# A decoder block's attention stage: the context's local sums and their rounded halves at another place in the step, and the integer transposes of the up projection at another place in the queue

## What is computed

```python
x = _layernorm(x + _L0_attn_ref(x, Wqkv, Wout, Wgate, bgate, decay_param))   # causal linear attention
x = _layernorm(x + _L0_xattn_ref(x, ctx_1024, ctx_1024))                     # decayed sum of ctx*ctx over the blocks
x = _layernorm(x + _L0_ffn_ref(x, w_gate, w_up, w_down))                     # quantised gated FFN
# _L0_attn_ref: q, k = elu + 1; running sums with a decay per head; out = q * running_kv / den;
#               g = sigmoid(out @ Wgate.T + b); (g * out + (1 - g) * v) @ Wout.T
# _L0_xattn_ref: r = 0.9 * r + (k * v)[t] along the first axis of (16, 512, 512); out = q * r
```

## Time and profile before

| | us |
|---|---|
| median of 3 runs | 2640.48 |
| lowest, highest | 2638.88, 2640.67 |
| profiled execution | 2641.53 |
| its span, first to last instruction | 2639.8 |
| TensorE busy (matmul) | 2550.7 (97%) |
| VectorE busy | 2020.0 (77%) |
| ScalarE busy | 1356.8 (51%) |
| mean granted TensorE clock | 0.983 of full |

### The profile page before, as it was taken

One profiled execution on the slowest core, in us unless ns is written; L12 is line 12 of the kernel. 1 busy time (PEld: TensorE's weight loads), 2 busy tenths in 40 slices (PEclk: granted clock), 3 DMA queues, 4 the chain that ended last, 5 costly groups with the idle time before them and its releaser, 6 DMA issues.

```text
span 2639.8 us, 32066 instructions
## 1 busy us (share of the span) xinstructions
PE 2550.7 (97%) x11218; PEld 2132.8 (81%) x11218; DVE 2020.0 (77%) x2838; ACT 1356.8 (51%) x1727; POOL 397.1 (15%) x281
## 2 busy tenths in 40 slices
PE   7999999999999997999999999999999699999998
PEld 6888888888888886888888887888888588888887
DVE  7899999999999895555555458987777766666665
ACT  4455555555555555333333358888888522222222
POOL 0000000000000000000000003422222143333332
PEclk9999999999999998999999999999999899999999
DMA  4011222211211224555555559777777635555552
GB/s 175 9 64 72 83 100 91 76 72 72 80 72 68 84 112 153 182 191 191 189 183 185 183 172 314 272 262 256 258 258 260 243 152 213 211 211 211 212 211 115
DMA packets 146714, 429.85 MB, mean 163 GB/s; under 512 B 73184, under 2 KB 81632, under 8 KB 106976
## 3 DMA queue, kind: packets, MB, share of 16 engines
q1 hardware_dynamic: 143920, 412.39, 43.0%
q10 hardware_dynamic: 2736, 16.78, 1.6%
HBM read 235.67 MB, written 177.21 MB: 156 GB/s over the span
## 4 chain that ended last, share of the span: by engine, by line
PE 57%; DVE 2%; DMA 1%; ACT 1%; issue 1%; SPq 0%; POOL 0%; POOLq 0%; ACTq 0%; DVEq 0%
PE pair L1999 12%; PE pair L2001 12%; PE pair L2000 12%; PE pair L2058 6%; PE pair L2059 6%; PE pair L2060 6%; DMA ff_q<-x_ints 0%; PE pair L2009 0%; DVE ff_gs L1722 0%; DMA ff_gs<-gate_ints 0%; DMA up_products<-ff_group 0%; DVE ff_up_max L1745 0%; DVE ff_up_abs L1727 0%; DVE ff_lo L1917 0%; ACT ff_group L1504 0%
## 5 line engine op out<-in xcount | busy, mean ns | idle before, releaser
L1999 PE MATMUL pair<-ff_hi,wide_h 128*128 128x512 f32 x1536 | 599.7, 390 | 3.0 <-ACT ff_group L1504 2.8
L2001 PE MATMUL pair<-ff_hi,wide_l 128*128 128x512 f32 x1536 | 598.3, 390 | 0.0
L2000 PE MATMUL pair<-ff_lo,wide_h 128*128 128x512 f32 x1536 | 598.3, 390 | 0.0
L1504 ACT ACTIVATE ff_group<-pair,ff_scales 128x512 f32<-128x512 f32 x384 | 257.2, 686 | 304.1 <-PE pair L2001 293.0
L1999 PEld LDWEIGHTS pair<-ff_hi,wide_h 128*128 128x128 f32 x1536 | 288.7, 188 | 64.2 <-ACT ff_group L1504 3.2
L2001 PEld LDWEIGHTS pair<-ff_hi,wide_l 128*128 128x128 f32 x1536 | 288.7, 188 | 60.4
L2000 PEld LDWEIGHTS pair<-ff_lo,wide_h 128*128 128x128 f32 x1536 | 288.7, 188 | 59.4
L2058 PE MATMUL pair<-wide_h,ff_hi 128*128 128x512 f32 x768 | 299.7, 390 | 24.4 <-DVE ff_lo L1911 23.5
L935 PE MATMUL pair<-xh,wide_h 128*128 128x512 f32 x768 | 309.2, 403 | 12.3 <-DVE wide_l L543 11.7
L939 PE MATMUL pair<-xh,wide_l 128*128 128x512 f32 x768 | 307.0, 400 | 0.0
L936 PE MATMUL pair<-xl,wide_h 128*128 128x512 f32 x768 | 306.7, 399 | 0.0
(11 more groups left out here) (235 smaller groups left out, 4622.6 us busy)
## 6 DMA issues: line engine op xcount, KB each, us to landing
gate_products<-ff_group SPq DMA_DIRECT2D x48, 1024.0 KB, 4.0
ff_raw<-gate_products SPq DMA_DIRECT2D x48, 1024.0 KB, 5.7
up_products<-ff_group SPq DMA_DIRECT2D x48, 1024.0 KB, 4.4
ff_raw<-up_products SPq DMA_DIRECT2D x48, 1024.0 KB, 9.2
gate_ints<-ff_gs SPq DMA_DIRECT2D x48, 512.0 KB, 2.7
ff_gs<-gate_ints SPq DMA_DIRECT2D x48, 512.0 KB, 9.9
xt_raw<-in_xT SPq DMA_DIRECT2D x64, 256.0 KB, 3.5
csq<-in_ctx_rows SPq DMA_DIRECT2D x16, 1024.0 KB, 7.3
```

What stands on the lines that cost most here:

```text
L1504: act.activation(group[:, g, m * T:(m + 1) * T], out_ps[(GM * g + m) % 6][:], ACT.Copy, scale=s_x).then_inc(evacuated, 1)
L1999: pe.matmul(o, wh[:, m, k], hi[:, par, k], start=(k == 0), stop=False)
L2000: pe.matmul(o, wh[:, m, k], lo[:, par, k], start=False, stop=False)
L2001: mm = pe.matmul(o, wl[:, m, k], hi[:, par, k], start=False, stop=(k == KC - 1))
```

## The change

On ScalarE the copy into `csq_h` goes from the middle of the step to its end, behind `normalise(0, s)`; the copy into `rec_turned` goes ahead of `split_x(s+1, (2, 3))`. On VectorE `local_sums(s+1)` goes from behind `split_x(s+1, (0, 1))` to behind `second_residual`, and `last_sum_low(s+1)` to the very end of the step, behind `scale_difference(s+1, 0)`. On TensorE `turn_reciprocals` goes three matmuls earlier in projection tile 3. On SyncE each up step used to issue the transpose for the next step at its group 0; now it issues the one for the step after next at its group 1, behind the store of the group's products. No arithmetic is added or removed, apart from two unread warm-up matmuls in step 0.

```diff
@@ scalar, step
                     if front:
-                        act.wait_ge(summed, (TT - 1) * (s + 1))
-                        if back:
-                            act.wait_ge(carry_ready, s)
-                        act.activation(csq_h[:], csq[:, 1 - par, TT - 1], ACT.Copy).then_inc(sqh_ready, 1)
+                        act.wait_ge(turned_ready, s + 1)
+                        act.activation(rec_turned[:], turn_bank, ACT.Copy).then_inc(rec_turned_ready, 1)
                     if nxt:
                         split_x(s + 1, (2, 3))
-                    if front:
-                        act.wait_ge(turned_ready, s + 1)
-                        act.activation(rec_turned[:], turn_bank, ACT.Copy).then_inc(rec_turned_ready, 1)
                     if back:
                         squares(0, s, (2, 3))
...
                     if back:
                         normalise(0, s)
+                    if front:
+                        act.wait_ge(summed, (TT - 1) * (s + 1))
+                        if back:
+                            act.wait_ge(carry_ready, s)
+                        act.activation(csq_h[:], csq[:, 1 - par, TT - 1], ACT.Copy).then_inc(sqh_ready, 1)
@@ vector, step
                     if nxt:
                         split_x(s + 1, (0, 1))
-                    if front:
-                        local_sums(s + 1, 1 - par)
...
                     if nxt:
                         split_x(s + 1, (2, 3))
-                    if front:
-                        last_sum_low(s + 1, 1 - par)
...
                     if back:
                         second_residual(s, par)
+                    if front:
+                        local_sums(s + 1, 1 - par)
                     if piece is not None and piece + 1 < NPIECE:
                         piece_scales(piece + 1)
                     if front:
                         scale_difference(s + 1, 0)
+                        last_sum_low(s + 1, 1 - par)
@@ tensor, step
-                        project(s, (3,), lambda k: turn_reciprocals(s) if k == 1 else None)
+                        project(s, (3,), lambda k: turn_reciprocals(s) if k == 0 else None)
...
-                        unread(20)
+                        unread(18)
                         turn_reciprocals(s)
@@ sync, ffn_phase
-                def up_step(b, par, ahead, turns=True):
+                def up_step(b, par, ahead, turn_at=1):
                     for g in range(NG):
                         t = NG * b + g
                         if ahead:
-                            if g == 0 and turns:
-                                turn_free(NB + b + 1, 1 - par, 16 * (NB // 2))
                             sp.wait_ge(sr_ready, t + 1)
                             load_gate(b + 1, g)
-                            if g == 0 and turns:
-                                turn(b + 1, 1 - par)
                         sp.wait_ge(gs_ready, t + 1)
                         sp.dma_start(gs_dram[b, g], gs16[:, g]).then_inc(gs_stored[g], 16)
+                        if g == turn_at:
+                            turn_free(NB + b + 2, par, 16 * (NB // 2))
                         sp.wait_ge(evacuated, GM * (NG * (NB + b) + g + 1))
                         sp.dma_start(up_dram[t], group[:, g]).then_inc(stored[g], 16)
+                        if g == turn_at:
+                            turn(b + 2, par)
```

More of the change, by code:

```diff
@@ L1317, in _ @@
                 turn(1, 1)
-                up_step(0, 0, True, turns=False)
+                up_step(0, 0, True)
                 load_weights(6)
                 load_weights(7)
-                with sp.Fori(0, (NB - 2) // 2) as i:
+                with sp.Fori(0, (NB - 4) // 2) as i:
                     for u in range(2):
                         up_step(2 * i + 1 + u, (1 + u) % 2, True)
-                up_step(NB - 1, 1, False)
+                up_step(NB - 3, 1, True)
+                up_step(NB - 2, 0, True, turn_at=None)
+                up_step(NB - 1, 1, False, turn_at=None)
                 def load_up_first(g):
```

## The result

| | before | after |
|---|---|---|
| median of 3 runs, us | 2640.48 | 2689.26 |
| lowest, highest | 2638.88, 2640.67 | 2686.99, 2694.79 |
| span of the profiled execution | 2639.8 | 2693.1 |
| mean granted clock, profiled execution | 0.983 | 0.978 |

Run against run on one chip, the changed kernel takes 1.0193 of the time before, with a 95% interval of [1.0178, 1.0207]; between the two medians it is 48.8 us more. No change at all is far outside the interval; whether the loss is more or less than 2% is not settled, since the interval holds 1.02. The prediction said 2691 us. The profiled execution is the longest of its three runs (2694.79 us); the other two had a granted clock of 0.982 and 0.983.

A forecast was written before the change was run, and what follows sets the result against it. TensorE, busy 97% of the span, was taken as the bound, with VectorE almost as full. Terms -1 + 50 + 6 - 4.5 = +50.5 us on a median of 2640.5 gave 2691 us, range 2662 to 2704.

The forecast's parts named there:

- the chain: Attention step: means, late local sums, csq_h copy, relu to tanh, scale_difference, then gate m = 2; step 62.3 us without clock loss.
- The wait for `xl`: Ahead of qkv(0) in each attention step: late tiles 2 and 3 leave TensorE idle for about 0.9 us.
- the wait at the gate: Ahead of gate m = 2: TensorE, ready at 376.6, waits 3.8 us for scale_difference, which ends at 380.4.
- the clock: Lower TensorE clock after idle time slows matmuls on the path by 1.7 us, taking the step from 62.3 to 64.0 us.
- At the second broadcast: Start of the attention phase: step 0's shorter broadcast wait and step 1's hardly waiting gate give -1 us.
- The last step: End of the attention phase: four copies between csq_h and the first tanh on ScalarE, +5 us, taken as +6 with clock.
- The SyncE part: Up steps: the earlier transpose removes TensorE's 2.8 us stop and 1.7 us of clock, -4.5 us, bounds 0 to -4.5.
- After 3.8 us I take it to fall in nearly every step: Attention steps: TensorE's clock falls after the gate m = 2 wait in nearly every step, 1.7 us each.
- the slack of 1.1 us: Kernel before: scale_difference ended at 317.14, TensorE reached gate m = 2 at 318.28, which hid the whole chain.
- The same chain without the clock: Rival: lower clock falls inside idle time or only ahead of gate m = 2; step 62.3 us, 2666 us; chance 0.15.
- More than forecast: Rival: two slow stretches in a row, or VectorE the bound behind gate m = 2; 2706 to 2714 us; chance 0.09.
- Faster: Rival: the tanh isn't late, the chain to scale_difference is hidden; -33 us, 2607 us; chance 0.04.

The follow-up runs named there:

- copy_behind_tanh: Changed kernel with ScalarE's copy into csq_h moved behind the next step's first tanh, low half following, sums still late: 2627.13 us, 0.9961 of the kernel before.
- sums_in_place: Changed kernel with the local sums back at their old place on VectorE, ahead of first_residual 2: 2628.93 us, 0.9961 of the kernel before.
- filled_wait: Changed kernel with 15 unread matmuls ahead of gate m = 2 on TensorE in steps 1 to 15: 2674.86 us, 1.0138 of the kernel before.
- sums_behind_sd1: Changed kernel with local sums behind the next step's scale_difference 1, csq_h copy behind the third tanh, low half behind the fourth result: 2641.06 us, 1.0006 of before.
- up_only: Kernel before with only the change's up_step, the transpose for the step after next at group 1: 2636.08 us, 0.9990 of the kernel before.
- early_only: Kernel before with tiles split early, sums behind the second split, rec_turned ahead of the csq_h copy, csq_l at step end: 2601.65 us, 0.9856 of before.
- sums_split: Changed kernel with two of three local sums in VectorE's idle time ahead of splitting tiles 2 and 3, csq_h copy behind the tanh: 2613.14 us, 0.9904 of before.
- up_as_before: Changed kernel with the old up_step, so the SyncE transpose order is undone: 2696.68 us, 1.0218 of the kernel before.

## Why the prediction was right

**The mechanism.** Every step of the chain stands in the rows: `rec_turned` is off the path, ScalarE waits 4.22 us for the sums (4.2 forecast), the means end at 323.2, the next step's tanh and `scale_difference` come behind the copy, and TensorE stops ahead of gate m = 2 and nowhere else in the gate. `copy_behind_tanh` shows that it is the waiting copy, by moving it, with the low half behind it; `sums_in_place` that without late sums the loss isn't there.

**The terms.** Steps 2 to 15 take (1016.91 - 58.06 - 61.0) / 14 = 64.13 us on average, forecast 64.0 (58.06 and 1016.91 are the starts of the first and the last broadcast, and 61.0 us is step 1). The wait for `xl` is about 1.1 us (forecast 0.9), the wait at the gate 3.4 us (forecast 3.8): `qkv(0)` starts 0.3 us later than forecast, on average 1.9 us behind the start of the projection's last matmul where 363.0 - 361.36 = 1.6 us was forecast, and what starts `qkv(0)` later shortens the other wait. Without the clock a step takes 62.6 us (`filled_wait`, and the three steps of the changed kernel that kept the clock), forecast 62.3; the clock adds 1.45 us on average, forecast 1.7. The two misses cancel. The sum over the phase hides two more. At the second broadcast the changed kernel is 121.30 - 119.10 = 2.2 us ahead, forecast 1. The fourteen steps behind it take 53.3 us more than before, forecast 50: the forecast set its 64.0 us against a mean of 60.44 us, while these fourteen took (965.80 - 121.30) / 14 = 60.3 us. The last step costs 6.3 us (forecast 6): the start of the last broadcast moved by 51.1 us and the end of the phase by 57.4. The SyncE part gave 4.1 us, forecast 4.5. Together 57.4 - 4.1 = 53.3 us between the profiled spans, and 48.8 between the medians, forecast 50.5. That the sum hits the median within 2 us is partly luck: the three runs of the changed kernel lie 7.8 us apart.

**A step that was wrong in detail.** "After 3.8 us I take it to fall in nearly every step" and "for 1.7 us" don't describe what happens. Of thirteen waits of 3.3 to 3.5 us, three were followed by no slow stretch (steps of 62.6 to 62.7 us), five by one (63.9 to 64.1), and after five TensorE was at the lower clock already at the wait's end, as at 138.00, where the first matmul takes 0.79 us instead of 0.50 (steps of 64.9 to 65.0). Only the mean came out near.

**A reading that was wrong beside the sum.** The prediction takes the tanh of before from the step at 302.32 (315.76 + 61.01 = 376.8), and from there also the slack of 1.1 us. But ahead of that tanh ScalarE stood idle for 1.35 us, waiting for TensorE, which a slow stretch had held up. In the step that the prediction follows there was no slow stretch ahead of gate m = 2, and the rows are (the last is the first matmul of m = 2):

```profile
375.32 0.65 ACT L416 ACTIVATE pair<-pair,half_bg 128x512 f32<-128x512 f32 x1
...
376.07 0.63 DVE L702 SCALAR_TENSOR_TENSOR att<-pair,att 128x512 f32<-128x512 f32 x1
...
377.49 0.39 PE L935 MATMUL pair<-ah,go_h 128*128 128x512 f32 x1
```

The slack was 377.49 - 376.70 = 0.8 us. Counted from the start of the projection's last matmul (361.36, and 310.45 in the changed kernel), the tanh came 17.9 - 14.0 = 3.9 us later, and TensorE was ready for m = 2 0.2 us earlier: 3.9 - 0.8 + 0.2 = 3.3 us, the wait that was measured. The forecast of 64.0 us uses neither number, since it adds up the new chain from the means.

**The rivals.** *The same chain without the clock* is wrong as a whole: filling the wait with work gave 14.4 us of the median, and 20.7 us between the profiled spans. The Trainium skill ("TensorE: Matmul & The Clock Gate", "What's actually happening") puts the ramp at the lower clock below 1% of a typical span for modelling. As a size the runs agree, 14 to 21 us are below 1% of 2690 us; but the whole change is 1.9%, and the sum without the clock was 2666 us. *More than forecast* holds in its first half for five steps of thirteen, not for all; its second half, VectorE as the bound, was seen in `sums_behind_sd1`, not here. *Faster*: with the copy out of the way (`copy_behind_tanh`) the result was 11 us below before, not the 33 us that this rival gave. It counted no wait at gate m = 2, where 10.0 us in all stay, and 0.9 us a step for `xl`, where 17.7 us in fifteen stay. These make some 14 of the 22 us that are missing; the rest isn't assigned.

**The transpose.** The queue was held for 9.89 us before and for 5.62 us after, and `up_only` shows a stall that was real: 4.3 us came back between the profiled executions, 2.3 us between the medians. The Trainium skill's 261 GB/s ("DMA: Bandwidth & Descriptors", "Latency and other measured facts") gives an estimate of 2.0 us for these 512 KB. The trace doesn't agree: from the transpose's issue at 1603.14 to ScalarE's read at 1615.16 it is 12.0 us, and ScalarE stood idle for 10.09 of them.

## What to carry to other kernels

Before putting a copy that waits for another engine at the end of an in-order list, count what stands behind it in the next iteration, and read how much slack its consumer has: here 0.8 us of slack stood against a tanh that came 3.9 us later. When a wait that is removed only uncovers the next one, look at what frees the buffers of that next one; splitting two tiles earlier, together with the order that goes with it, was worth 36.5 us (`early_only`), most of what TensorE had been idle or slowed for in the attention phase (24.2 us of waits and 17.3 us of clock). Where two engines are both nearly full, as VectorE and TensorE here, the place to try first for moved work is the second engine's idle time, 1.78 us a step here: `sums_split`, which uses it, was 14 us shorter than `copy_behind_tanh`, which leaves it unused.

## What the runs showed of the hardware

Idle time on TensorE cost more than itself, and by varying amounts. The waits of 0.98 to 1.22 us ahead of `qkv(0)` had no slow stretch behind them in the changed kernel. The two that were longer had, the one of 1.78 us in step 0 (at 60.34) and one of 1.79 us. Behind the latter the gate's wait is 1.6 us shorter than its neighbours, so what the lower clock took from `qkv(0)` the wait gave back.

```profile
507.26 0.49 PE L934 MATMUL pair<-xh,wide_h 128*128 128x512 f32 x1 [1.79 <-DVE xl L575]
524.52 0.50 PE L934 MATMUL pair<-ah,go_h 128*128 128x512 f32 x1 [1.77 <-DVE att L702]
```

Thirteen waits of 3.33 to 3.48 us, alike within 0.15 us, showed nothing, one slow stretch, or a clock at the lower level (1.2 GHz) from their end on, at no cost, about 1.4 and about 2.3 us a step; the three windows above had a granted clock of 1.00, 0.72 and 0.54. What decides between the three isn't shown by any run here. It is not drawn anew in every step: the profiled execution of `up_as_before`, whose attention phase has the same order, goes through the same sequence, each of its fourteen steps within 0.2 us of the one here. Yet the changed kernel's three executions lie 7.8 us apart, at granted clocks of 0.978 to 0.983, while the four of `filled_wait`, whose profiled one kept the clock at 1.00 in these steps, lie within 1.4 us. Unread matmuls in place of the idle time made a kernel with 210 more matmuls in fourteen steps about 14 us faster (2674.86 against 2689.26 us).
